# The cross products of a triangular solve parted by heads, and the order of five engines changed around them

## The reference

```
k = k / max(norm(k), 1e-12)
def step(S, (k, v, q, a, b)):
    v_old = S @ k
    S = clip(a * S + b * outer(v - a * v_old, k), -5, 5)
    return S, S @ q
```

## Time and profile before

| | us |
|---|---|
| three executions | 1992.31, 1996.38, 1981.5; median 1992.31 |
| the profiled execution | 1995.18 |
| its span, first to last instruction | 1993.6 |
| PE busy in the span | 1675.7 (84%) |
| DVE busy | 1389.3 (70%) |
| POOL busy | 1098.4 (55%) |
| ACT busy | 878.3 (44%) |

### The profile page before, as it was taken

One profiled execution on the slowest core, in us unless ns is written; L12 is line 12 of the kernel. 1 busy time (PEld: TensorE's weight loads), 2 busy tenths in 40 slices (PEclk: granted clock), 3 DMA queues, 4 the chain that ended last, 5 costly groups with the idle time before them and its releaser, 6 DMA issues. The chain is left out here.

```text
span 1993.6 us, 59490 instructions
## 1 busy us (share of the span) xinstructions
PE 1675.7 (84%) x24752; PEld 1159.7 (58%) x24752; DVE 1389.3 (70%) x1884; ACT 878.3 (44%) x1762; POOL 1098.4 (55%) x1363
## 2 busy tenths in 40 slices
PE   7468899899889889889898988945998849999994
PEld 4235556566565565565665556635887746666652
DVE  5367688888889788888888786447788474443341
ACT  4336456555555555655655555313335132222221
POOL 0085586677668568668667767117345005555553
PEclk9678899999999889999989897777999869999997
DMA  3301222222222222222222212236332154444443
GB/s 123 88 24 34 53 66 55 64 66 66 64 76 57 60 68 62 68 56 65 64 55 67 54 45 55 60 109 242 128 127 95 53 213 95 87 81 87 84 84 40
DMA packets 89031, 156.53 MB, mean 79 GB/s; under 512 B 15676, under 2 KB 54084, under 8 KB 87564
## 3 DMA queue, kind: packets, MB, share of 16 engines
q1 hardware_dynamic: 72860, 124.76, 21.4%
q0 software_dynamic: 15904, 27.93, 7.5%
HBM read 112.53 MB, written 40.12 MB: 77 GB/s over the span
## 5 line engine op out<-in xcount | busy, mean ns | idle before, releaser
L1169 PE MATMUL d_ps<-hT,turn_shared 128*128 128x512 f32 x768 | 411.4, 643 | 28.3 <-DMA d_cw<-convp_in 10.4
L817 POOL TENSOR_TENSOR turn_shared<-turn_shared,d_tmp 128x31 f32<-128x31 f32 (+15 forms) x496 | 290.9, 586 | 38.9
L812 POOL TENSOR_TENSOR d_tmp<-turn_shared 128x31 f32<-128x31 f32 (+15 forms) x496 | 284.9, 574 | 38.9
L882 DVE SCALAR_TENSOR_TENSOR turn_shared<-d_ps,d_cw,turn_shared 128x1023 f32<-128x1023 f32 (+2 forms) x192 | 243.9, 1271 | 6.1 <-ACT turn_shared L601 3.8
L1169 PEld LDWEIGHTS d_ps<-hT,turn_shared 128*128 128x128 f32 x768 | 128.3, 195 | 112.2 <-issue 75.7
L2236 POOL DMA_INDIRECT out<-m_yo,m_slot_i x71 | 113.4, 1597 | 134.2 <-DVE m_yo L2336 99.6
L2215 ACT ACTIVATE m_hm<-m_ps,m_b_tile 128x128 f32<-128x128 f32 x284 | 81.2, 368 | 229.6 <-PE m_ps L2384 226.7
L659 ACT ACTIVATE d_S<-d_S,gamma_chunk 128x64 f32<-128x64 f32 x448 | 130.0, 339 | 81.7 <-DVE d_S L910 74.5
L650 ACT ACTIVATE d_U<-d_ps 128x128 f32<-128x128 f32 x256 | 70.0, 273 | 196.6 <-PE d_ps L1379 193.3
L829 POOL TENSOR_TENSOR d_Z<-d_um,d_kmax 128x1024 f32<-128x1024 f32 x32 | 62.6, 1956 | 160.7 <-PE d_ps L1320 160.7
L2374 PE MATMUL m_ps<-m_w,m_xs 128*128 x284 | 138.8, 612 | 10.9 <-issue 10.3
(11 more groups left out here) (239 smaller groups left out, 3702.0 us busy)
## 6 DMA issues: line engine op xcount, KB each, us to landing
turn_shared<-steps_scratch SPq DMA_DIRECT2D x64, 256.0 KB, 3.9
d_qg<-gamma_scratch SPq DMA_DIRECT2D x64, 256.0 KB, 4.7
y_scratch<-d_yT SPq DMA_DIRECT2D x256, 64.0 KB, 1.8
d_arow<-ab_scratch SPq DMA_DIRECT2D x128, 128.0 KB, 3.0
y<-y_scratch SPq DMA_DIRECT2D x8, 2048.0 KB, 8.3
m_w<-w_in SPq DMA_DIRECT2D x16, 512.0 KB, 10.5
turn_shared<-x_in SPq DMA_DIRECT2D x4, 1024.0 KB, 11.2
turn_shared<-x_by_half_in SPq DMA_DIRECT2D x8, 512.0 KB, 6.9
```

What stands on the lines that cost most here:

```text
L812: nc.gpsimd.tensor_tensor(tv, Tq[:, s + 1:, s].rearrange("p (r a) -> p r a", a=1).broadcast_to([P, left, known]), X[:, s, 0:known].rearran ...
L817: nc.gpsimd.tensor_tensor(X[:, s + 1:, 0:known], X[:, s + 1:, 0:known], tv, ALU.subtract).then_inc(s_sub, 1)
L882: nc.vector.scalar_tensor_tensor(out=dst[:, j + 1:], in0=src[:, 0:T - 1 - j], scalar=cw[:, u // BP % 2, n, 2 - j:3 - j], in1=dst[:, j + 1: ...
L1169: return nc.tensor.matmul(dst[:, g, :], w[:, m % 2, n, dc, :], hT[:, dc, at:at + G], start=(dc == 0), stop=(dc == DC - 1))
```

## The change

`cross_first`, `cross_second`, `keep_cross_first` and `keep_cross` take the head `k` as an argument: where one call made the products of both heads (64 of 32 x 32), two calls make 32 each. Their semaphores count two for a turn. Within a call the products now go round two places of TensorE's array (b2 = 0, 1), where they went round four (k = 0, 1 by b2 = 0, 1).

```
-            def cross_first(u):
-                pe.wait_ge(s_xn, u + 1)
-                if u:
-                    pe.wait_ge(s_x2, u)
+            def cross_first(u, k):
+                if k == 0:
+                    pe.wait_ge(s_xn, u + 1)
+                    if u:
+                        pe.wait_ge(s_x2, 2 * u)
                 for n in range(NCW):
-                    for k in range(2):
-                        for b2 in range(2):
-                            last = nc.tensor.matmul(cross_at(b2, k * NCW + n, 1), TTx[quad(b2, 0), k * NCW + n, :],
-                                                    Xn[quad(b2, 0), k * NCW + n, :], start=True, stop=True)
+                    for b2 in range(2):
+                        last = nc.tensor.matmul(cross_at(b2, k * NCW + n, 1), TTx[quad(b2, 0), k * NCW + n, :],
+                                                Xn[quad(b2, 0), k * NCW + n, :], start=True, stop=True)
                 last.then_inc(s_p1, 1)
...
-            def keep_cross_first(u):
-                act.wait_ge(s_p1, u + 1)
-                for k in range(2):
-                    for b2 in range(2):
-                        last = nc.scalar.activation(P1[quad(b2, 1), heads_of(k), :], cross_half(b2, k, 1), ACT.Identity)
+            def keep_cross_first(u, k):
+                act.wait_ge(s_p1, 2 * u + k + 1)
+                for b2 in range(2):
+                    last = nc.scalar.activation(P1[quad(b2, 1), heads_of(k), :], cross_half(b2, k, 1), ACT.Identity)
                 last.then_inc(s_pe, 1)
```

The lists of calls are written anew for all engines. The number of instructions of each kind stays the same. Of the loops:

```
                 if chain:
+                    gamma_k(tc)
                     decay_k(tc, 0)
                     decay_k(tc, 1)
                     decay_k(tc, 2)
+                    decay_k(tc, 3)
+                if bound:
+                    bound_terms(tb, 0)
                 if prep:
                     clear_x(u)
                     solve(u)
-                if chain:
-                    decay_k(tc, 3)
-                if prep:
-                    gamma_k(u)
```

On DVE the calls between the end of one solve and the start of the next change so (L1033 and L1027 turn the solve's result, L994 is `largest_k`, L1021 `scale_v`):

```
-                        solve_matrix(un, 0)
-                        solve_matrix(un, 1)
-                    if prep and c == 14:
-                        largest_k(u)
-                        scale_v(u, 1)
-                    if new_k and c == 14:
-                        turn_matrix(un)
...
                     if prep and c == 0:
+                        solve_matrix(u, 0)
+                        solve_matrix(u, 1)
+                    if bound and c == 0:
+                        update_max(tb, 2)
+                    if chain and c == 0:
+                        scale_v(tc, 1)
+                    if prep and c == 0:
+                        turn_matrix(u)
...
+                    if chain and c == 12:
+                        turn_y(tc, 2)
+                    if prep and c == 12:
                         rows_of_x(u)
                         turn_x(u)
...
+                    if prep and c == 14:
+                        largest_k(u)
+                    if bound and c == 14:
                         bound_scan(tb, 1)
                         bound_max(tb, 1)
```

More of the change, by code:

```diff
@@ L1090, in _ @@
                         tap_v(u, 0, 2)
-                    if bound and c == 4:
-                        turn_y(tb, 3)
+                    if chain and c == 4:
+                        turn_y(tc, 0)
                     if prep and c == 4:
                         decayed_q(u)
-                    if chain and c == 4:
+                    if chain and c == 5:
                         update_max(tc, 0)
@@ L1467, in _ @@
-                    if prep and c == 4:
-                        proj_v(u, 1, 2)
+                        proj_q(u, 1, 1)
+                        proj_q(u, 1, 2)
+                    if bound and c == 2:
+                        y_of_u(tb, 7)
+                    if chain and c == 3:
+                        y_of_u(tc, 0)
+                    if chain and c == 4:
+                        y_of_u(tc, 1)
                     if prep and c == 5:
-                        kq(u, 0)
+                        proj_v(u, 1, 3)
@@ L1471, in _ @@
                     if chain and c == 6:
-                        y_of_u(tc, 0)
+                        y_of_u(tc, 2)
                     if chain and c == 7:
-                        y_of_state(tc, 1, 1)
+                        y_of_state(tc, 3, 0)
                     if chain and c == 8:
-                        y_of_state(tc, 2, 1)
-                        y_of_u(tc, 2)
-                    if prep and c == 9:
-                        v_turned(u, 0)
+                        y_of_u(tc, 3)
@@ L1480, in _ @@
+                    if new_k and c == 9:
+                        proj_k(un, 0, 1)
                     if chain and c == 10:
-                        y_of_u(tc, 3)
-                    if new_k and c == 11:
-                        proj_k(un, 1, 1)
-                    if prep and c == 12:
-                        cross_first(u)
-                    if chain and c == 12:
-                        y_of_state(tc, 4, 0)
-                    if chain and c == 13:
-                        y_of_state(tc, 5, 1)
@@ L1490, in _ @@
-                    if prep and c == 14:
+                        y_of_state(tc, 4, 1)
+                    if chain and c == 11:
+                        y_of_state(tc, 5, 1)
+                    if new_k and c == 12:
+                        proj_k(un, 1, 0)
+                    if new_k and c == 13:
+                        proj_k(un, 1, 2)
+                    if chain and c == 13:
+                        y_of_state(tc, 6, 1)
+                    if new_k and c == 13:
+                        proj_k(un, 1, 3)
@@ L1491, in _ @@
+                    if prep and c == 13:
+                        cross_first(u, 0)
+                    if prep and c == 15:
                         w_product(u, 0)
-                    if chain and c == 14:
-                        y_of_state(tc, 6, 0)
+                        seed_u(u, 0)
+                    if chain and c == 15:
+                        y_of_u(tc, 6)
                     if new_k and c == 15:
+                        kk(un, 0)
+                        kk(un, 1)
                         proj_q(un, 0, 0)
@@ L1542, in _ @@
                         seed_u(tc, 7)
-                        y_of_state(tc, 1, 0)
-                    if chain and c == 7:
-                        y_of_u(tc, 1)
                     if prep and c == 7:
                         kq(u, 1)
-                    if bound and c == 7:
+                    if chain and c == 7:
+                        seed_u(tc, 8)
+                        y_of_state(tc, 3, 1)
+                    if bound and c == 8:
                         z_turned(tb, 0)
-                    if new_k and c == 7:
+                    if new_k and c == 8:
@@ L1576, in _ @@
                     if chain and c == 12:
-                        y_of_state(tc, 4, 1)
-                        y_of_u(tc, 4)
                         seed_u(tc, 13)
-                        y_of_state(tc, 5, 0)
-                    if chain and c == 13:
-                        y_of_u(tc, 5)
+                        y_of_state(tc, 6, 0)
                     if prep and c == 13:
-                        cross_second(u)
+                        cross_first(u, 1)
                     if chain and c == 13:
@@ L1586, in _ @@
                         seed_u(tc, 14)
-                    if bound and c == 13:
-                        z_turned(tb, 1)
-                    if chain and c == 14:
-                        y_of_state(tc, 6, 1)
-                    if new_k and c == 14:
-                        kk(un, 0)
-                        kk(un, 1)
+                    if prep and c == 14:
+                        cross_second(u, 0)
                     if chain and c == 14:
                         seed_u(tc, 15)
+                    if prep and c == 14:
+                        cross_second(u, 1)
@@ L1596, in _ @@
+                    if bound and c == 14:
+                        z_turned(tb, 1)
             pe.wait_ge(s_mx, 2 * TURNS + 3)
```

234 lines of the change are left out of this document (110 added, 124 removed).

## The result

The changed kernel is slower by half a per cent: 1999.73 us (median of 17 executions, 1994.3 to 2006.96) against 1988.88 (17, 1981.5 to 1998.3), ratio 1.0048 with a 95% interval of 1.0033 to 1.0063. Run again beside the experiments it gave 1.0052 (1.0029 to 1.0075). The forecast was 1978 us, a gain; the change went the other way, within the 1% called "the same".

The account below looks back on a forecast made before the run. Bound: a ring of 15 gaps and 16 solves, the gap being DVE's work plus waits for PE. Terms 25.2 + 0.7 + 1.0 + 1.3 = 28.2 against 29.1 us, times 15 = -14 us: 1978 us, range 1944 to 2014.

Parts of the forecast that it names:

- the gap: Time from a solve's end on POOL to the next solve's start: 29.1 us in the mean, forecast 28.2.
- (1): DVE's own work in the gap, with 0.5 us of wait for `join`: 25.5 - 0.8 + 0.5 = 25.2 us.
- (2): DVE's wait ahead of the scans, 1.51 us: counted as gone, since `largest_k` makes DVE arrive 2.2 us later.
- (5): First cross product on PE, slower over two places: DVE's wait for the state of chunk 13 is 1.3 us, 0 to 3.
- (3): DVE's wait for `kk` in the gap, 1.27 us before: forecast 0.7 us, between 0 and 1.6.
- (4): Lag of the gap's start behind the solve's end, from PE's +1.6 us of work ahead: 1.0 us, 0 to 3.
- C: Rival: splitting the cross products on PE is free, 8.6 ns a record; -26 us, 1966 us, chance 0.10.
- the ring: Solve and gap in turn, each solve needing results of the one before: 15 gaps and 16 solves, period 72.2 us.
- (6): POOL, ACT and SP: their reordered work costs nothing, covered by 10 us and more of idle time in the gap.
- Rival A: The waits for PE in the gap vanish and DVE's row remains: gap 26.0 us, -46 us, 1946 us, chance 0.30.
- Rival B: PE becomes late for the cross products: gap 30.7 us, +24 us, 2016 us, chance 0.18.
- The stalls called "issue": PE stops inside the second cross product, 7 times, 11.4 us in all; the half as dense runs should end them.

Follow-up runs that it names:

- e10: e5 with `largest_k` put back behind `solve_matrix` and `update_max`, as in the kernel before: 1993.52 us, ratio 1.0011 to the kernel before.
- e2: Changed kernel with each cross product again one call of 128 records round four places: 1982.12 us, ratio 0.9954 to the kernel before.
- e5: e2 with both halves of ScalarE's `silu_q` moved behind `keep_u` of chunk 4: 1956.03 us, ratio 0.9810 to the kernel before.
- e3: Kernel before with only the loop order inside both cross products changed, one call going round two places: 2010.08 us, ratio 1.0097.
- e7: e5 with `cross_first` behind `state_sum` of chunk 13 instead of ahead of it: 1957.15 us, ratio 0.9818 to the kernel before.
- e6: Changed kernel with only ScalarE's `silu_q` moved behind `keep_u` of chunk 4: 1975.56 us, ratio 0.9924 to the kernel before.
- e1: The changed kernel run again, unedited, beside the experiments: 2000.94 us, ratio 1.0052 to the kernel before.
- e8: e5 with `largest_k` moved out of the gap into chunk 9 of the solve: 2161.24 us, ratio 1.0852 to the kernel before.
- e9: e5 with `join` waiting by halves of `solve_matrix` and `scale_v` put behind `scalars`: 2012.38 us, ratio 1.0110 to the kernel before.
- e12: e2 with one PE projection, `proj_v(u, 1, 1)`, put ahead of `state_sum` of chunk 4: 1961.01 us, ratio 0.9875 to the kernel before.

## Why the prediction was wrong

The frame held: time is 15 gaps and 16 solves, the solve is untouched, and DVE's row with its waits makes the gap. In the order of the steps (own work, `join`, scan, `kk`, lag, state) the forecast gap was 24.7 + 0.5 + 0 + 0.7 + 1.0 + 1.3 = 28.2 us; measured it is 24.5 + 0.85 + 0.99 + 0.97 + 1.32 + 1.04 = 29.7. Two thirds of the miss is the scan's wait. The last turn's 3.4 us stood in no term. The steps, by their numbers:

(1) *DVE's own work* was right in size: in the gap shown there are 28.65 us from `rows_of_x` (799.83) to the next solve, of which 0.97, 1.23, 0.81 and 1.18 are waits; 24.5 us are left, 24.7 were forecast. (The 25.05 us of the stretch include 0.8 of `state` and `turn_y` ahead of `rows_of_x`, which here are the whole lag.) It was wrong in one sentence: `largest_k` moved within the gap "nothing is gained by itself". e10 shows 2.8 us a gap in the mended kernel. The wait for `join` and `v_turned` was 0.85 us, in the range, over the 0.5 taken.

(2) *The scan's wait* is the first step that failed. It was counted as gone and measured 0.99 us, as before (0.98). The condition was written beside it ("only if PE is more than about 2 us late"), and that is what came: z_turned ends 2.35 us later than before (15.77 against 13.42 us behind the solve's end). Nor was the cover 2.2 us: step (1) had moved `turn_y` and a `state` away from ahead of the scan, 0.8 us that step (2) did not take off; from `rows_of_x` DVE reaches the scan 1.15 us later (13.50 against 12.35). Step (5) held what makes PE late: two calls at the lower clock. I had priced the pitch at full clock (2.2 us a turn) and written "most of it is hidden". It is 2.9 us a turn (3.6 + 2.5 against 1.8 + 1.3; for the first product the same view has 37.1 us for 1906 records after and 20.0 for 1920 in e2), and the delay of z_turned could have been summed then: the second product runs behind a wait for ScalarE, so at the lower level. e2 shows what this one term is worth: the wait goes to 0.03, and the time to 1982.

(3) *kk* 0.97 us, 0.7 forecast, in the range. 

(4) *The lag* was 1.32 us in the mean, near to the 1.0 forecast, but for another reason: that term came out by luck. I had summed PE's work and compared it with its idle time; e5 has all of that work and a lag of 0.05. The failing step is the sum itself: it was made on PE alone, and the second edit that counts, silu_q together with a bare `state_sum` of chunk 4, is on ScalarE and PE together.

(5) *The state of chunk 13* 1.04 us, against 1.3. The pitch was right: 64 records in 1.20 us, 17 ns a record forecast, (1.20 - 0.2) / 64 = 16 ns measured (0.2 us for the last record, the estimate of the prediction). C, the split for free, is out. By the rule of the Trainium skill named there ("TensorE: Matmul & The Clock Gate", Part 3, "What overlaps and what doesn't": a weight load overlaps only when the row group differs), both orders would cost the same, and the two runs e2 and e3 speak against it for these 32 x 32 products. Hardly anything of the ring hangs on the chunk's own wait (e7).

(6) *POOL, ACT and SP at nothing*: this is the second step that failed, and the larger one. The argument was that ScalarE is busy only 18.53 of 29.6 us in the gap. What ScalarE's order costs together with PE's is 25 us (e6 against e1), by one block of 3.3 us in front of one copy of 0.25 us, and it lies in the solve and not in the gap. In the sum it hides in the lag of step (4), which had 1.0 us for another cause.

Rival A (1946, the waits vanish) did not come true for the changed kernel. It is near to e5, with both causes mended: a gap of 26.7 us, where A said 26.0, and 1956 us; but DVE's waits for PE have not vanished there (`scale_v` 1.03, `kk` 0.75, state 0.47 us). Rival B had the right sign and for the changed kernel the right kind of mechanism (PE late for z_turned at the lower clock, a lag that falls and rises with it) but not the size: 2016 against 1999.7, since its sum put the whole of the extra work on the path. The stalls called "issue" did go, 11.4 us at the second cross product. e3 had fewer of them there than the kernel before (L1340: 3.8 against 11.4 us) and was 18 us slower, so they are worth less than the places; what they are worth alone no run shows, nor that instruction supply causes them.

What stays open: why the clock falls behind the 1.47 us in five of 13 turns and not in the others, and how the 35 us by which the mended order beats the kernel before divide: e10 takes them all back by the place of `largest_k`, but in an order where all four `decay_k` stand ahead of the solve.

## What to carry to other kernels

When a change reorders several engines, go through the waits between each pair of neighbours in both new lists, in the middle of the long stretch too, and not only where the ring closes: the busy share of an engine says nothing about one block of 3 us in front of a copy of 0.3 us. Price a moved step by everything that waits for it, through every engine's queue: who else must it wait for (e8), what stands behind its readers (e10, e9). And if small products are parted, part them so that each half still goes round as many places of the array as the whole (not shown here: e2 put them back into one group).

## What the runs showed of the hardware

- Records of 32 x 32 products (two for each product) that go round two places of the array come one every 16 ns at full clock, round four every 8.6 ns, with 0.2 us taken off a group for its last record; the mean time of one record is the same (229 and 227 ns). Halving a group of 128 records that way makes two groups nearly as long as the whole (1.20 us each, against 1.29; at the lower level 1.92 each, against 1.93). One group of 128 over two places (e3) takes 2.12 us.
- A wait of 1.47 us of PE is not always followed by the lower level: in the same place, with the same wait, two projections took 1.98 us in some turns and 3.45 in others. Without it (waits of 0.42 us or less there) the clock of the solve stayed at full level in all 28 solves of turns 2 to 15 of e5 and e12, though PE stood still for 0.8 to 1.4 us at a later place in 13 of them.
- The solve on POOL took 43.29 us in the mean in e5 and 42.95 in e1, with the same instructions: 0.3 us over 16 solves are 5 us that e5 gives back. It is neither ScalarE's order alone (e10, with that of e5, has 43.0) nor the faster ring alone (e12, 43.0). No run here shows why.
